# A four-stage sequence kernel on one core: the last two chunks put in another order on four engines, the key norms of three rows in one batch, the pair products split into steps

## What is computed

```python
# second attention: a scan over the 4 batch rows, for each token apart
def step(S, kvq):                       # S: 32 blocks of 8 x 8 per token
    k_norm = k_t / (norm(k_t) + 1e-6)
    delta = v_t - einsum('bnij,bnj->bni', S, k_norm)
    S_new = tanh(S + einsum('bni,bnj->bnij', delta, k_norm))
    Sq = einsum('bnij,bnj->bni', S_new, q_t)
    return S_new, Sq * silu(Sq)
x = layernorm(x + scan(x))
# second feed-forward: mixes each token with the one ahead of it
xr, xk = mu_r * x + (1 - mu_r) * x_prev, mu_k * x + (1 - mu_k) * x_prev
out = sigmoid(xr @ W_r.T) * (square(relu(xk @ W_k.T)) @ W_v.T)
x = layernorm(x + out)
```

## Time and profile before

| | |
|---|---|
| median of 3 runs | 1185.43 us (1184.94 to 1185.73) |
| the profiled execution | 1184.52 us |
| its span, first to last instruction | 1182.7 us |
| last DVE instruction of `last_mix` ends | 1180.18 us |
| first DVE instruction on rows of the last chunk (L2144) | 1060.15 us |
| PE, DVE, ACT, POOL busy | 1083.8, 965.1, 606.7, 483.6 us |
| DVE idle between 1067 and 1183 us, waiting for others | 26 us, in pieces of up to 6.84 us |

### The profile page before, as it was taken

The page is one execution under the profiler, slowest core; times in us unless marked ns, Lnnn a source line. Parts: engine busy times, 40 slices in busy tenths (PEclk is TensorE's granted clock), DMA queues, the critical chain, the costliest instruction groups (busy, mean ns, idle before and its releaser), DMA issues.

```text
span 1182.7 us, 16467 instructions
## 1 busy us (share of the span) xinstructions
PE 1083.8 (92%) x5761; PEld 837.7 (71%) x5761; DVE 965.1 (82%) x1417; ACT 606.7 (51%) x1039; POOL 483.6 (41%) x379
## 2 busy tenths in 40 slices
PE   6999999999999999999999999999999999984434
PEld 3666666677787777788778778877877887772323
DVE  3688888872045998998899899899989989999883
ACT  1345555554345356555735655573565557344552
POOL 1366677774333234344324433432343343231220
PEclk9999999999999999999999999999999999998657
DMA  6334544753522431332333133233313323310000
GB/s 227 128 138 159 190 174 176 275 189 110 175 90 72 134 97 52 110 111 85 95 101 126 44 115 101 94 91 98 130 40 120 96 82 90 95 48 0 0 18 21
DMA packets 45339, 127.02 MB, mean 107 GB/s; under 512 B 4320, under 2 KB 21472, under 8 KB 43104
## 3 DMA queue, kind: packets, MB, share of 16 engines
q1 hardware_dynamic: 44416, 114.72, 30.3%
q10 hardware_dynamic: 864, 11.54, 2.6%
...
## 4 chain that ended last, share of the span: by engine, by line
DVE 55%; PE 25%; issue 9%; ACT 6%; POOL 2%; DMA 1%; DVEq 0%; ACTq 0%; POOLq 0%; SPq 0%
DVE tmp L2015 7%; PE lower L441 7%; PE lower L1164 6%; DVE tmp L2005 6%; DVE Sq L2007 5%; DVE tmp L2021 4%; DVE delta L2017 4%; PE bank L1164 3%; DVE stats L142 2%; PE lower L541 2%; DVE delta L2019 2%; DVE S L2023 2%; ACT look L646 1%; DVE whole L1967 1%; PE bank L471 1%
## 5 line engine op out<-in xcount | busy, mean ns | idle before, releaser
L1830 POOL TENSOR_TENSOR a_lo<-whole,a_hi 128x512 fp32r<-128x512 f32 x128 | 181.8, 1438 | 268.3 <-ACT a_hi L1467 197.1
L1164 PE MATMUL lower<-b_hi,ring 128*128 128x512 f32 x512 | 193.6, 396 | 1.4 <-ACT a_hi L1467 1.4
L1164 PE MATMUL lower<-b_lo,ring 128*128 128x512 f32 x512 | 190.7, 390 | 1.7 <-POOL b_lo L1830 1.7
L1164 PE MATMUL lower<-a_hi,ring 128*128 128x512 f32 x496 | 186.3, 394 | 1.7 <-issue 1.7
L1164 PE MATMUL lower<-a_lo,ring 128*128 128x512 f32 x496 | 184.2, 390 | 0.2 <-POOL a_lo L1830 0.2
L1830 POOL TENSOR_TENSOR b_lo<-whole,b_hi 128x512 fp32r<-128x512 f32 x64 | 93.9, 1474 | 145.1 <-ACT b_hi L1467 145.1
L1450 ACT ACTIVATE S<-S 128x1024 f32<-128x1024 f32 x56 | 58.6, 1059 | 183.0 <-DVE S L2023 183.0
L1466 ACT ACTIVATE whole<-lower,hs 128x512 f32<-128x512 f32 x126 | 86.2, 684 | 76.8 <-PE lower L1164 71.8
L441 PE MATMUL lower<-wa,xT 128*128 128x512 f32 x240 | 111.2, 608 | 10.9 <-DMA wa<-wa_dram 8.0
L1164 PEld LDWEIGHTS lower<-b_hi,ring 128*128 128x128 f32 x512 | 96.2, 188 | 21.9 <-issue 1.8
L1164 PEld LDWEIGHTS lower<-b_lo,ring 128*128 128x128 f32 x512 | 96.0, 188 | 22.0 <-POOL b_lo L1830 2.3
...
## 6 DMA issues: line engine op xcount, KB each, us to landing
ring<-ffn_copy_dram SPq DMA_DIRECT2D x128, 512.0 KB, 3.6
...
```

The source lines that it names most:

```text
L1164: ins = nc.tensor.matmul(out, a, b, start=(first and n == 0), stop=(last and n == len(pairs) - 1))
L1830: nc.gpsimd.tensor_tensor(lo[:, m, :], t["whole"][:, m % 4, :], hi[:, m, :].bitcast(F32), ALU.subtract).then_inc(lo_done, 1)
```

## The change

Only `finish()` and the last store change; the number of products and their sizes are the same.

- Row 1's keys, values and queries go to banks 6 and 7, and row 3's too. PE waits for all four turned rows before row 1 (before: two), and for the copy of the row two before it. The wait of the first state's second half for row 1 is gone.
- `norms_of` runs for row 0, then once for rows 1 to 3 (before: row 1, then rows 2 and 3). It waits for the copies of all four rows.
- PE's `mix_pair` is split into `turn_pair`, `pair_products` and `pair_values`, so that the rows of pair 3 are transposed between the products and the values of pair 2.
- ACT's `add_rows` is split into sums and `add_squares`; `key_acts` gives its last step to `mix_gates`. The small copy of a column in `turned_pair` moves ahead of the wait for PE.
- The layer norm of x3 rows 0-1 (chunk 7) comes ahead of that of y4 (chunk 6) on ACT and POOL. `read_q(0, 1)` comes after the first root on POOL.
- The order of calls changes on ACT, POOL and DVE. `gate_rows` waits for `pair_y4`, since x3 is overwritten there. The last store has a semaphore of its own.

```diff
                     def scan_row(b):
-                        lo = (4, 2, 4, 4)[b]
-                        if b == 2:
-                            pe.wait_ge(fin_kvq, 2)
-                        elif b == 3:
-                            pe.wait_ge(fin_kvq, 6)
-                        pe.wait_ge(fin_turned, b + 1)
+                        lo = (4, 6, 4, 6)[b]
+                        if b >= 2:
+                            pe.wait_ge(fin_kvq, 2 * b - 2)
+                        pe.wait_ge(fin_turned, BATCH if b else 1)
...
-                    for g, (c, n) in enumerate(PAIRS_LEFT):
-                        mix_pair(g, n)
+                    for g in range(2):
+                        turn_pair(g, g)
+                        pair_products(g, g)
+                        pair_values(g, g)
+                    turn_pair(2, 0)
+                    pair_products(2, 0)
+                    turn_pair(3, 1)
+                    pair_values(2, 0)
+                    pair_products(3, 1)
+                    pair_values(3, 1)
...
                     kvq_row(2)
+                    kvq_row(3)
...
-                    kvq_row(3)
                     add_rows(0, x3, range(BATCH), ln3_steps, d * N_LN3 + 2)
+                    add_squares(0, x3, range(BATCH))
                     state_tanh(1, 0)
...
+                    state_tanh(1, 1)
                     turned_pair(0, 0)
-                    state_tanh(1, 1)
+                    state_tanh(2, 0)
                     key_acts(0, 0)
-                    turned_pair(1, 1)
-                    state_tanh(2, 0)
-                    key_acts(1, 1)
+                    mix_gates(0, 0)
                     state_tanh(2, 1)
                     gate_parts(slice(0, 2), 4)
-                    add_rows(1, y4, range(BATCH), pair_y4, 2)
-                    add_rows(2, x3, range(0, 2), fin_x3, 1)
+                    turned_pair(1, 1)
+                    state_tanh(3, 0)
+                    key_acts(1, 1)
+                    add_rows(1, x3, range(0, 2), fin_x3, 1)
+                    mix_gates(1, 1)
+                    add_squares(1, x3, range(0, 2))
+                    state_tanh(3, 1)
                     act.wait_ge(fin_rs, 2)
+                    scaled_rows(x3, range(0, 2), t["rstd3"], t["shift3"], pair_norm3)
+                    add_rows(2, y4, range(BATCH), pair_y4, 2)
+                    gate_parts(slice(2, 3), 6)
+                    turned_pair(2, 0)
+                    add_squares(2, y4, range(BATCH))
+                    gate_parts(slice(3, 4), 8)
+                    act.wait_ge(fin_rs, 3)
                     scaled_rows(y4, range(0, 2), t["rstd4"], t["shift4"], pair_out)
                     scaled_rows(y4, range(2, 4), t["rstd4"], t["shift4"], pair_out)
-                    act.wait_ge(fin_rs, 3)
-                    scaled_rows(x3, range(0, 2), t["rstd3"], t["shift3"], pair_norm3)
-                    state_tanh(3, 0)
-                    turned_pair(2, 0)
-                    state_tanh(3, 1)
-                    gate_parts(slice(2, 3), 6)
                     key_acts(2, 0)
-                    gate_parts(slice(3, 4), 8)
                     act.wait_ge(rs4, LAST - 1 + 1)
                     act.wait_ge(fin_sq, 2 * BATCH)
                     scaled_rows(x3, range(2, 4), t["rstd3"], t["shift3"], pair_norm3, out=x1in)
+                    mix_gates(2, 0)
+                    turned_pair(3, 1)
+                    key_acts(3, 1)
+                    mix_gates(3, 1)
                     act.wait_ge(rs4, LAST - 1 + 2)
                     scaled_rows(y4, range(0, 2), t["rstd4"], t["shift4"], pair_out)
-                    turned_pair(3, 1)
-                    key_acts(3, 1)
...
                     read_q(0, 0)
-                    read_q(0, 1)
                     added_mean(0, every)
                     added_root(0, every, t["rstd4"], t["shift4"])
+                    read_q(0, 1)
                     read_q(1, 0)
                     read_q(1, 1)
                     read_q(2, 0)
+                    added_mean(1, front)
                     read_q(2, 1)
-                    added_mean(1, every)
-                    added_root(1, every, t["rstd4"], t["shift4"])
-                    added_mean(2, front)
-                    added_root(2, front, t["rstd3"], t["shift3"])
+                    added_root(1, front, t["rstd3"], t["shift3"])
+                    added_mean(2, every)
+                    added_root(2, every, t["rstd4"], t["shift4"])
...
                     earlier_x3()
-                    norms_of(slice(1, 2))
+                    norms_of(slice(1, BATCH))
                     earlier_gate()
                     next_state(0, 0)
                     next_state(0, 1)
                     read_sums(0)
-                    norms_of(slice(2, BATCH))
+                    next_state(1, 0)
                     mix_pair(0, 0)
-                    next_state(1, 0)
-                    mix_pair(1, 1)
                     next_state(1, 1)
-                    mixed_pair(0, 0)
                     read_sums(1)
                     next_state(2, 0)
+                    mix_pair(1, 1)
+                    mixed_pair(0, 0)
+                    gate_rows(front, 2, 1)
+                    next_state(2, 1)
                     mixed_pair(1, 1)
-                    gate_rows(front, 2)
-                    next_state(2, 1)
                     read_sums(2)
                     last_read(0)
+                    last_read(1)
                     mix_pair(2, 0)
-                    last_read(1)
-                    gate_rows(back, 6)
+                    gate_rows(back, 6, 2)
                     moments_of(x3, back, t["mv3"], fin_x3, 2)
+                    mix_pair(3, 1)
                     mixed_pair(2, 0)
                     moments_of(y4, front, t["mv4"], pair_y4, 3)
-                    mix_pair(3, 1)
```

43 lines of the change are left out of this document (27 added, 16 removed).

## The result

| | us |
|---|---|
| changed kernel, median of 5 | 1167.85 (1165.52 to 1168.15) |
| kernel before, median of 5, same chip | 1184.94 (1184.25 to 1185.73) |
| ratio | 0.9847, 95% interval 0.9836 to 0.9858 |
| forecast | 1165.6, range 1162 to 1171 |
| profiled execution and its span | 1167.29 and 1165.4 |

Two more measurements of the same kernel beside the experiments gave 1166.99 (ratio 0.9846, 0.9833 to 0.9858) and 1166.83 (0.9858, 0.9843 to 0.9873). The change is faster by 1.3 to 1.7% over the three intervals, and its own executions lie up to 3 us apart. That spread turns out to be the most useful thing in this case.

What follows compares the result with a forecast made beforehand. DVE, nearly always at work, bounds the kernel up to `mix_pair(2, 0)`; then chunk 7's two pairs pass PE, ACT and DVE one behind the other. 11.0 + 8.8 = 19.8 us off 1185.43 gives 1165.6, range 1162 to 1171.

Steps and rivals of the forecast that it cites:

- Part 1: DVE up to the second norms: without the wait for row 1, these start at 1078.8 us instead of 1079.58.
- Part 2: Key norms on DVE: one batch of three rows takes 6.4 us, between ends of 5.3 and 9.5.
- Part 3: DVE's work up to `mix_pair(2, 0)`: without waits this starts at 1137.9 instead of 1148.87, 11.0 us earlier.
- (c): DVE's `mixed_pair(1, 1)` at 1129.5: PE's values for it are ready at 1129.0, the tightest place by 0.5 us.
- (d): ACT's parts of pair 2 ahead of `mix_pair(2, 0)`: 1.6 us at most, even without gain from the norms' new order.
- Part 4: The last two pairs, from `mix_pair(2, 0)` to DVE's end: 22.5 us instead of 31.3, 8.8 us saved.
- The last three products: PE ahead of `last_mix`: 6.4 us taken, between 5.3 at high clock and 7.6; level not fixed by the order.
- the gate without its wait: DVE's gate of rows 2-3 of chunk 7, behind `mix_pair(2, 0)`: silu is ready, so the 4.6 us wait goes.
- (A): Chunk 7's pairs stay one behind the other, ACT waiting for y4's stores: 1174.4 us with all 8.8 lost; chance 0.12.
- (B): GpSimd holds up DVE instructions in `finish()`: two or three hits cost 3 us, giving 1168.6; chance 0.06.
- (C): Slower than before: late `x1in` holds up both pairs on strictly ordered PE; 1189 us if 24 us late; chance 0.04.
- (D): The change does nothing that counts, stalls are only renamed: 1185 us; chance 0.02.

Runs made afterwards that it cites:

- third trace: Trace of the changed kernel measured a third time, nothing edited, all rows of the last chunk at 2.4 GHz: 1166.83 us, ratio 0.9858.
- y4 first: Changed kernel with the norm of y4 (chunk 6) again ahead of that of x3 rows 0-1 on ACT and POOL: 1170.98 us, ratio 0.9884.
- values first: Changed kernel with PE's value product of pair 2 again ahead of the transposes of pair 3: 1166.64 us, ratio 0.9844.

## Why the prediction was right, point by point

**Part 1, the start of the joined norms: the one mis-sized term.** The prediction said 1078.8 us, 11.99 behind the common point. It came at 14.98. The step that failed is "its keys and values are there after two thirds of 2.85 us": durations of PE at 2.4 GHz were taken for all four rows, and the closing words "this term can only cost if ACT is late" left out PE. At 1.2 GHz in part, row 0 cost 1.0 us more (a wait of 1.33 instead of 0.34 ahead of the first norms) and rows 1 to 3 made DVE wait 2.15. With the rows at 2.4 GHz (third trace) the norms start at 11.96. The uncertainty of the clock was weighed for the last products and not here, where joining the norms had just made PE's third row something that DVE waits for.

**Part 2, the norms:** 6.4 us forecast, 1087.74 - 1081.31 = 6.43 measured. The step of 1.1 us for a row held, and nothing else of the batch grows. The worth of joining, 3.1, held as well in the trace at 2.4 GHz.

**Part 3, DVE up to mix 2:** from the gate of chunk 6 it should take 1137.9 - 1085.2 = 52.7 us; it took 1140.61 - 1087.74 = 52.87, without a wait. The place named as tightest, (c), held: the values of pair 1 were over at 1130.47 and `mixed_pair(1, 1)` came at 1132.23. Place (d) held only because of the new order of the two norms: "y4 first" shows that without it the cost is 5.4 us and not 1.6, since the start of the norm of y4 was counted from the wrong instruction. The conclusion was right, the bound behind it was not.

**Part 4, from mix 2 to the end:** 22.5 us forecast, 22.26 measured, by two errors that cancel. The last three products took 5.45 us (1151.74 to 1157.19), all at the high level, where 6.4 had been taken between the ends 5.3 and 7.6; the forecast had left their level open, and that one error covers the other is luck; and DVE started 1.05 us behind them because it had to leave the branch, which nothing in the forecast had. Before, that time lay under the 6.84 us for PE. By steps, the 9.05 us gained between mix 2 and the end are 7.06 from mix 2 to the gate (8.63 to 1.57, the 4.6 us wait and the last read that stood between), 0.91 from the gate to mix 3 (9.54 to 8.63) and 1.09 from there to `last_mix` (8.52 to 7.43). Most of the gain is the gate's wait. The prediction had both parts of it, the gate without its wait and the transposes that fit in behind the gate products "at next to no wait"; it put `x1in` at 1145.1 and the end of the gates at 1145.0, as close together as they came out. The place of the transposes is worth 0.55 us of it ("values first").

`x1in` came at 1147.59, 5.41 behind the gate, where 5.6 had been taken:

```profile
1146.52 1.07 ACT L1645 ACTIVATE x1in<-x,shift,rstd 128x256 f32<-128x256 f32 x2
```

**The rivals.** (A), stores in the way of pair 3: no wait of ACT for them shows; mix 3 came 10.2 us behind mix 2. (B), GpSimd holding DVE up: no DVE instruction of 1024 columns took over 1.23 us from the joined norms on. It happened the other way round. POOL's mean of four columns took 1.08 us, where the same size took 0.23 at 1093.84:

```profile
1136.04 1.08 POOL L1912 TENSOR_SCALAR mean<-mv 128x4 f32<-128x4 f32 x1 [2.95 <-ACT y L1691]
```

It began 0.23 us behind a DVE product with two inputs from SBUF (1135.81 to 1137.03) and ended 0.09 behind it. SBUF — State Buffer of the Trainium skill (section on the two separate sides) says that whichever of the two starts first holds the port pair for its whole instruction; the trace agrees, and here DVE was first. It cost nothing, since y4's mean had time. (C) and (D) did not occur.

**The sum.** Forecast 19.8 us less, measured 17.1 (1184.94 to 1167.85), 18.3 and 17.3 in the other two measurements. In the first trace the end came at 96.54 where 93.6 was forecast. In the trace with all rows at 2.4 GHz it is 94.01, so 2.5 us of the 2.9 go with the clock in the rows.
